# The start of an attention kernel: condition loaded first, its sigmoid from an exponential and a reciprocal, its factor on ScalarE

## The reference, cut to what matters

```
tf    = sigmoid(sum(cond, -1))
decay = exp(-exp(w)) * (0.5 + 0.5 * tf)
ek    = exp(min(f, 30));  ekv = ek * f
a forward and a backward scan  a = a * decay + ekv,  b = b * decay + ek
num   = nf + nb - ekv + euk * f;   den = df + db - ek + euk     with euk = exp(min(u + f, 30))
out   = sigmoid(x) * (num / max(den, 1e-8)) * (0.8 + 0.2 * tf)
```

## Time and profile before

| | us |
|---|---|
| median of 3 runs | 692.53 (692.39 to 693.21) |
| the profiled execution | 689.73 |
| its span, first to last instruction | 687.9 |
| TensorE busy in the span | 541.2 |
| VectorE busy | 407.4 |
| ScalarE busy | 373.0 |
| GpSimd busy | 147.5 |
| from the span's start to the first product of the attention | 33.88 |
| from the span's start to the first maxima | 48.04 |

### The profile page before, as it was taken

The page is one execution under the profiler, slowest core; times in us unless marked ns, Lnnn a source line. Parts: engine busy times, 40 slices in busy tenths (PEclk is TensorE's granted clock), DMA queues, the critical chain, the costliest instruction groups (busy, mean ns, idle before and its releaser), DMA issues.

```text
span 687.9 us, 13927 instructions
## 1 busy us (share of the span) xinstructions
PE 541.2 (79%) x5668; PEld 392.5 (57%) x5668; DVE 407.4 (59%) x612; ACT 373.0 (54%) x794; POOL 147.5 (21%) x115
## 2 busy tenths in 40 slices
PE   0097769778687766578999999999649999999980
PEld 0054445556455642353664656667648999996560
DVE  5889999999997477966655544454831111111223
ACT  6987788978876407555657555666322222222112
POOL 1000000000000127732019555520021222223110
PEclk9995699878868999899999999999759999999995
DMA  9500000000001000000000000000269999888825
GB/s 350 189 1 1 1 1 1 2 1 1 1 1 32 1 0 1 0 1 1 2 2 2 3 2 2 3 2 3 69 256 423 420 420 361 333 330 304 338 95 191
DMA packets 18480, 71.38 MB, mean 104 GB/s; under 512 B 4849, under 2 KB 9969, under 8 KB 14705
## 3 DMA queue, kind: packets, MB, share of 16 engines
q1 hardware_dynamic: 15408, 64.20, 24.5%
q0 software_dynamic: 1920, 5.25, 2.0%
q10 hardware_dynamic: 1088, 1.05, 0.5%
HBM read 65.77 MB, written 4.72 MB: 102 GB/s over the span
## 4 chain that ended last, share of the span: by engine, by line
PE 52%; DVE 31%; ACT 8%; issue 4%; DMA 3%; POOL 1%; SPq 0%; ACTq 0%; DVEq 0%; POOLq 0%
PE PS L1442 39%; DVE arena L942 4%; DVE nmx L1029 4%; DVE arena L939 4%; PE PS L1948 2%; PE PS L2017 2%; PE PS L1724 1%; PE PS L1589 1%; DVE R L956 1%; DVE arena L953 1%; DVE arena L954 1%; DMA arena<-in_moe 1%; DVE arena L948 1%; DVE arena L949 1%; ACT arena L773 1%
## 5 line engine op out<-in xcount | busy, mean ns | idle before, releaser
L1442 PE MATMUL PS<-arena 128*128 128x128 f32 (+6 forms) x1376 | 156.9, 291 | 17.6 <-DVE arena L1126 11.4
L1442 PEld LDWEIGHTS PS<-arena 128*128 128x128 f32 (+4 forms) x1376 | 125.8, 164 | 41.9 <-issue 25.0
L611 ACT ACTIVATE arena<-PS,nmx 128x128 f32<-128x128 f32 (+1 forms) x128 | 52.0, 422 | 32.6 <-DVE nmx L1029 32.6
L1390 DVE TENSOR_TENSOR R<-arena,PS 128x128 f32<-128x128 f32 x16 | 4.6, 288 | 88.1 <-ACT arena L870 88.1
L389 POOL TENSOR_SCALAR arena<-ident,gcol 128x128 f32<-128x128 f32 x4 | 2.4, 602 | 220.2 <-DMA gcol<-in_gcol 220.2
L449 POOL TENSOR_TENSOR arena<-arena 128x1024 f32<-128x1024 f32 x16 | 37.8, 2367 | 40.6 <-DVE arena L1208 32.5
L1506 PE MATMUL PS<-arena 32*128 32x128 f32 (+1 forms) x128 | 22.9, 438 | 29.9 <-ACT arena L611 29.6
L481 POOL DMA_INDIRECT ypair<-arena,oid x20 | 19.8, 988 | 121.8 <-ACT arena L876 121.8
L1442 PE MATMUL PS<-arena,R 128*128 128x256 f32 x192 | 44.2, 380 | 0.6 <-ACT arena L876 0.6
L1442 PEld LDWEIGHTS PS<-arena,R 128*128 128x128 f32 x192 | 35.2, 190 | 5.1 <-issue 1.0
L942 DVE TENSOR_TENSOR_SCAN arena<-dmat,arena 128x1023 f32<-128x1023 f32 x16 | 37.6, 2348 | 0.6
(11 more groups left out here) (306 smaller groups left out, 1198.3 us busy)
## 6 DMA issues: line engine op xcount, KB each, us to landing
arena<-in_moe SPq DMA_DIRECT2D x23, 1408.0 KB, 8.2
arena<-in_moe SPq DMA_DIRECT2D x23, 768.0 KB, 9.7
inproj<-in_inproj SPq DMA_DIRECT2D x1, 1344.0 KB, 10.5
arena<-in_fT SPq DMA_DIRECT2D x1, 1024.0 KB, 5.0
xT<-in_xT SPq DMA_DIRECT2D x1, 1024.0 KB, 5.4
R<-in_w1T SPq DMA_DIRECT2D x1, 1024.0 KB, 7.4
R<-in_w2T SPq DMA_DIRECT2D x1, 1024.0 KB, 9.4
R<-in_w3T SPq DMA_DIRECT2D x1, 1024.0 KB, 11.5
```

Source lines behind the costliest of these rows:

```text
L611: sc.activation(pr[u % 2][:, j, 0:n], PS[:, 2 * (u % 2) + j // 2, (j % 2) * 256:(j % 2) * 256 + n], ACT.Exp, bias=nmx[:, u % 2, j:j + 1], ...
L1442: last = mm(dst, l, r, start=(n == 0), stop=(n == len(pairs) - 1))
```

## The change

- **Loads.** `condT` is loaded first, with a semaphore of its own; `fT` comes in two loads, one for each half, with a semaphore each; `xT` goes behind the three feed-forward weights. `wu` is issued from ScalarE's queue, as the first thing in its program. `ones` and `notfirst` are not loaded any more: VectorE writes them with memsets, and also `tiny`, ahead of all its other work.
- **Sigmoid of the condition.** ScalarE takes `exp(-sum)`, in the table set of exponential and logarithm, which is now the first one loaded; VectorE adds one and takes the reciprocal.
- **First inputs.** The minimum with 30 is taken by half, behind `dq`. `fc = f * cb` is made by ScalarE (`by_condition`), two copies scaled by `cb` for each half. The scaled inputs of the first denominator scan (`ekq` of i = 0) are made by VectorE (`first_input`) instead of ScalarE's four copies.
- **ScalarE's order.** Decay of gate 0, exponential and factor of half 0, scaled values, bonus(0), exponential and factor of half 1, absolute sum 0, guess(0), absolute sum 1, the sigmoid's table, sigmoid of half 0, absolute sum 2, sigmoid of half 1, decay(1), scaled inputs (1,0), the three tanh, the queries, and only behind these the table of exponential and logarithm, the logarithm of `wtmp`, bonus(1) and the scaled inputs (1,1). The absolute sums write their unused output to `spent_abs`, words of the arena that the queries take later.
- **Names.** `pe_cond` and `pe_wsum` become `pe_sum` (1 and 2), `dve_ln` becomes the second count of `dve_winv`, `pool_pad` and `pool_diag` become `pool_made`.

```diff
-            load(fT, a["fT"], "f")
-            load(wu[:], a["wu"], "small")
-            load(condT[:], a["condT"], "small")
-            load(ones[:], a["ones"], "small")
-            load(notfirst[:], a["notfirst"], "small")
-            load(xT[:], a["xT"], "x")
+            load(condT[:], a["condT"], "cond")
+            load(fT[:, 0, :], a["fT"][:, 0, :], "f")
+            load(fT[:, 1, :], a["fT"][:, 1, :], "f1")
 
             for w, n in enumerate(("w1T", "w2T", "w3T")):
                 load(R[:, 1 + w].rearrange("p c n -> p (c n)"), a[n], "ffn")
+            load(xT[:], a["xT"], "x")
...
-            sc.preload_act_table(ACT.Sigmoid)
-            act.wait_ge(S["pe_cond"], 1)
-            sc.activation(tf[:], bank(7, B), ACT.Sigmoid).then_inc(S["act_cond"], 1)
+            act.dma_start(wu[:], a["wu"]).then_inc(ld["small"], 16)
             sc.preload_act_table_set(LN_EXP)
-            act.wait_ge(ld["small"], 64)
+            act.wait_ge(S["pe_sum"], 1)
+            sc.activation(tf[:], bank(7, B), ACT.Exp, scale=-1.0).then_inc(S["act_cond"], 1)
+            act.wait_ge(ld["small"], 16)
...
-            for ct in range(CT):
-                act.wait_ge(S["dve_fmin"], ct + 1)
-                sc.activation(ek[:, ct, :], ek[:, ct, :], ACT.Exp).then_inc(S["act_ek"], 1)
-                if ct == 0:
-                    scaled_inputs(0, 0)
-                decay(ct)
-                if ct == 0:
-                    scaled_inputs(0, 1)
+            def exp_inputs(c):
+                act.wait_ge(S["dve_fmin"], c + 1)
+                sc.activation(ek[:, c, :], ek[:, c, :], ACT.Exp).then_inc(S["act_ek"], 1)
+
+            def by_condition(c):
+                f4, s4 = (w[:, c, :].rearrange("p (a b t) -> p a b t", a=CT, b=B // NCH) for w in (fc, fT))
+                for b in range(B // NCH):
+                    last = sc.activation(f4[:, :, b, :], s4[:, :, b, :], ACT.Copy, scale=cb[:, 2 * c + b:2 * c + b + 1])
+                last.then_inc(S["act_ek"], 1)
...
-            bonus(0)
-            scaled_inputs(1, 0)
-            reciprocal_guess(0)
-
-            act.wait_ge(ld["ffn"], 48)
-            for w in range(3):
-                done(sc.activation(A[:].rearrange("p a n -> p (a n)"), R[:, 1 + w].rearrange("p c n -> p (c n)"), ACT.Abs,
-                                   accum_out=wabs[:, w:w + 1]), "act_wabs")
+            def absolute_sum(w):
+                done(sc.activation(spent_abs, R[:, 1 + w].rearrange("p c n -> p (c n)"), ACT.Abs, accum_out=wabs[:, w:w + 1]), "act_wabs")
...
-
+            decay(0)
+            exp_inputs(0)
+            by_condition(0)
+            act.wait_ge(S["dve_dec"], 2)
+            scaled_inputs(0, 1)
+            bonus(0)
+            exp_inputs(1)
+            by_condition(1)
+            act.wait_ge(ld["ffn"], 48)
+            absolute_sum(0)
+            reciprocal_guess(0)
+            absolute_sum(1)
+            sc.preload_act_table(ACT.Sigmoid)
             sigmoid_x(0, 0)
+            absolute_sum(2)
             sigmoid_x(0, 1)
-
+            decay(1)
+            scaled_inputs(1, 0)
             act.wait_ge(S["dve_winv"], 1)
             for w in range(3):
                 wv = R[:, 1 + w].rearrange("p c n -> p (c n)")
                 sc.activation(wv, wv, ACT.Tanh, scale=winv[:, w:w + 1]).then_inc(S["act_tanh"], 1)
-            sc.preload_act_table_set(LN_EXP)
-
-            act.wait_ge(S["dve_ln"], 1)
-            sc.activation(wat[:], wtmp[:], ACT.Ln).then_inc(S["act_atanh"], 1)
-            bonus(1)
-            scaled_inputs(1, 1)
             act.wait_ge(ld["attn"], 48)
...
             for mt in range(CT):
                 queries(0, mt, mt)
+            sc.preload_act_table_set(LN_EXP)
+            act.wait_ge(S["dve_winv"], 2)
+            sc.activation(wat[:], wtmp[:], ACT.Ln).then_inc(S["act_atanh"], 1)
+            bonus(1)
+            scaled_inputs(1, 1)
...
+            done(v.memset(ones[:], 1.0))
+            done(v.memset(notfirst[:], 1.0))
+            done(v.memset(notfirst[:, 0:1], 0.0), "dve_ones")
...
             dve.wait_ge(S["act_cond"], 1)
+            done(v.tensor_scalar(tf[:], tf[:], 1.0, None, ALU.add))
+            done(v.reciprocal(tf[:], tf[:]))
             done(v.tensor_scalar(hf[:], tf[:], 0.5, 0.5, ALU.mult, ALU.add))
             done(v.tensor_scalar(cb[:], tf[:], 0.2, 0.8, ALU.mult, ALU.add))
+            dve.wait_ge(S["act_exw"], 1)
...
+            smallest(0)
             done(v.reciprocal(rdq[:], dq[:]))
...
+            smallest(1)
+
+            def values_in(c):
+                dve.wait_ge(S["act_ek"], 2 * c + 2)
                 done(v.tensor_tensor(ekv[:, c, :], ek[:, c, :], fc[:, c, :], ALU.mult), "dve_fc")
+
+            def first_input():
+
+                dve.wait_ge(S["act_ek"], 1)
+                by_batch = [P, CT, B // NCH, T]
+                done(v.tensor_tensor(ekq.rearrange("p (a b t) -> p a b t", a=CT, b=B // NCH),
+                                     ek[:, 0, :].rearrange("p (a b t) -> p a b t", a=CT, b=B // NCH),
+                                     dq[:, 0, :, 0:B // NCH].unsqueeze(3).broadcast_to(by_batch), ALU.mult))
...
-            inputs(0)
+            first_input()
+            values_in(0)
...
-            inputs(1)
+            values_in(1)
```

More of the change, by code:

```diff
@@ L277, in bank @@
             return PS[:, i, 0:n]
-        ld = {k: sem("ld_" + k) for k in ("x", "f", "const", "small", "ffn", "attn", "ssd", "gb", "route")}
+        ld = {k: sem("ld_" + k) for k in ("x", "f", "f1", "cond", "const", "small", "ffn", "attn", "ssd", "gb", "route")}
         ld_ring = [sem(f"ld_ring{i}") for i in range(RING)]
@@ L389, in _ @@
                     last = pool.tensor_scalar(diagg[:, ct, l, :], ident[:], gcol[:, ct, l:l + 1], None, ALU.mult)
-            last.then_inc(S["pool_diag"], 1)
+            last.then_inc(S["pool_made"], 1)
             def roots(c):
@@ L899, in _, with smallest @@
             v = nc.vector
-            dve.wait_ge(ld["f"], 16)
-            for ct in range(CT):
-                done(v.tensor_scalar(ek[:, ct, :], fT[:, ct, :], 30.0, None, ALU.min), "dve_fmin")
-            dve.wait_ge(S["act_exw"], 1)
+            done(v.memset(ones[:], 1.0))
+            done(v.memset(notfirst[:], 1.0))
+            done(v.memset(notfirst[:, 0:1], 0.0), "dve_ones")
+            done(v.memset(tiny[:, 0:1], -1e-8))
+            done(v.memset(tiny[:, 1:2], 1e-8))
+            def smallest(c):
+                dve.wait_ge(ld[("f", "f1")[c]], 16)
+                done(v.tensor_scalar(ek[:, c, :], fT[:, c, :], 30.0, None, ALU.min), "dve_fmin")
             dve.wait_ge(S["act_cond"], 1)
+            done(v.tensor_scalar(tf[:], tf[:], 1.0, None, ALU.add))
+            done(v.reciprocal(tf[:], tf[:]))
             done(v.tensor_scalar(hf[:], tf[:], 0.5, 0.5, ALU.mult, ALU.add))
             done(v.tensor_scalar(cb[:], tf[:], 0.2, 0.8, ALU.mult, ALU.add))
+            dve.wait_ge(S["act_exw"], 1)
             done(v.tensor_tensor(dec[:], ew[:].unsqueeze(3).broadcast_to([P, 4, CT, B]),
@@ L913, in _ @@
             done(v.tensor_scalar(dq[:], dq[:], 1e-12, None, ALU.max), "dve_dec")
+            smallest(0)
             done(v.reciprocal(rdq[:], dq[:]))
-            done(v.memset(tiny[:, 0:1], -1e-8))
-            done(v.memset(tiny[:, 1:2], 1e-8))
-            dve.wait_ge(ld["small"], 64)
-            def tiles(w):
-                return w.rearrange("p (a b t) -> p a b t", a=CT, b=B // NCH)
-            def inputs(c):
-                bs = slice(c * B // NCH, (c + 1) * B // NCH)
-                done(v.tensor_tensor(tiles(fc[:, c, :]), tiles(fT[:, c, :]),
-                                     cb[:, bs].unsqueeze(1).unsqueeze(3).broadcast_to([P, CT, B // NCH, T]), ALU.mult))
-                dve.wait_ge(S["act_ek"], c + 1)
-                done(v.tensor_tensor(ekv[:, c, :], ek[:, c, :], fc[:, c, :], ALU.mult), "dve_fc")
+            smallest(1)
+            def values_in(c):
+                dve.wait_ge(S["act_ek"], 2 * c + 2)
+                done(v.tensor_tensor(ekv[:, c, :], ek[:, c, :], fc[:, c, :], ALU.mult), "dve_fc")
+            def first_input():
[4 more added lines that the diff above has]
+                                     dq[:, 0, :, 0:B // NCH].unsqueeze(3).broadcast_to(by_batch), ALU.mult))
             def gate_step(i, k):
@@ L970, in ternary_scales @@
                 done(v.tensor_scalar(wsc[:], wsc[:], 1.0, None, ALU.add))
-                done(v.tensor_tensor(wtmp[:], wtmp[:], wsc[:], ALU.mult), "dve_ln")
+                done(v.tensor_tensor(wtmp[:], wtmp[:], wsc[:], ALU.mult), "dve_winv")
             def keys(c, mt, b):
@@ L1445, in acc @@
                 return last
-            pe.wait_ge(ld["small"], 64)
-            acc(bank(7, B), [(ones[0:64, :], condT[:, :])], "pe_cond")
+            pe.wait_ge(ld["cond"], 16)
+            pe.wait_ge(S["dve_ones"], 1)
+            acc(bank(7, B), [(ones[0:64, :], condT[:, :])], "pe_sum")
             pe.wait_ge(S["act_wabs"], 3)
```

(4 more changed lines are left out.)

28 lines of the change are left out of this document (16 added, 12 removed).

## The result

The changed kernel has a median of 685.64 us over 7 runs (683.52 to 686.96); the kernel before, run beside it, 692.39 over 7 (688.95 to 693.21). The ratio is 0.991, with a 95% interval of 0.9884 to 0.9935: faster by 4.5 to 8.0 us. I had forecast 688.0 with a range from 686.4, so the time fell out of the range, on the fast side. The profiled executions took 684.17 after (span 682.3) and 689.73 before.

A forecast was written before the change was run, and what follows sets the result against it. VectorE's order of work was taken to set the attention, with everything changed in series ahead of it. First scan 3.2 us earlier plus stalls of 0.55 and 0.80 made 4.5 us: median 692.53 - 4.5 = 688.0, range 686.4 to 690.2.

The forecast's parts named there:

- What limits the kernel, and that a gain reaches the end: VectorE's order sets the attention; a microsecond saved before the first maxima at 48.04 is one off the end.
- Part 1: Condition at the kernel's start: `condT` issued first lands at 3.3, `dec` is done at 5.25 against 9.8 before.
- I take 3.3: Landing time of `condT` at the start, taken nearest to where data first flows at the full rate.
- The rule that I set beside it: Fixed DMA cost of about 2.0 us puts `condT` at 2.7: sum 0.6 better, median 687.4.
- the rival of a late condition: At the start, `condT` lands at 5.0 or `wu` at 5.2: 688.7 to 689.7, chance 0.11.
- parts 1 to 3: From the condition to gate (0,0): first scan 3.2 us earlier, stalls of 0.55 and 0.80 gone, 4.5 us in all.
- Parts 2 to 4: First inputs to first maxima: scan at 10.6, both stalls gone, products to maxima unchanged, maxima at 43.5; sum 4.5 us.
- the rival with a switch of twice that: ScalarE's table switch ahead of bonus(1) and `weigh(0)` costs twice 1.30, `weigh(0)` 1.2 late: 689.2, chance 0.03.
- The carrying to the median: At the end: the 4.5 us summed in the profiled execution is subtracted from the median 692.53, giving 688.0.
- the load, the pace and the table: Range terms: `condT` at 2.3 (1.0) or late, two more slow TensorE products (0.9), ScalarE's table switch (689.2).

The follow-up runs named there:

- e3: The changed kernel with `condT` loaded third, behind both halves of `fT`: median 688.39 us, ratio 0.9969 to the kernel before.
- e5: The changed kernel with ScalarE's old order of work; loads, condition and first inputs stay changed: median 688.37 us, ratio 0.9965 to the kernel before.
- e1: The kernel before, run again without edits: median 690.57 us, ratio 1.0003.
- e14: The kernel before with 12 unused products on TensorE behind the condition's sum: median 687.55 us, ratio 0.9957.
- e11: The changed kernel with 12 unused products on TensorE right behind the condition's sum, early: median 680.35 us, ratio 0.9834 to the kernel before.
- e6: The changed kernel with 12 unused products on TensorE shortly ahead of the gate, between 22.4 and 28.6 us: median 680.80 us, ratio 0.9857 to the kernel before.
- e9: The kernel of e6 once more, unchanged: median 678.18 us, ratio 0.9832 to the kernel before.
- e10: The kernel of e6 with ScalarE's scaled inputs (1,1) moved behind the first weights, `weigh(0)`: median 680.30 us, ratio 0.9847 to the kernel before.
- e13: The kernel of e11 with 64 unused products in place of 12, so 256 extra instructions: median 684.88 us, ratio 0.9922 to the kernel before.
- e8: The changed kernel with `ekv` of half 0 made by GpSimd, ScalarE's bonus(0) and second exponential ahead of its scaled values: median 685.62 us, ratio 0.9927 to before.

## Why the prediction was wrong

**What limits the kernel, and that a gain reaches the end.** Right: the 5.14 at the maxima came out in full, as 5.8 to 6.75 between medians side by side; e3's 3.3 at the condition were 3.7 in the median, e5's 2.95 at the maxima about 3.

**Part 1, a gain too small.** The failed step inside the sum is "I take 3.3" for the landing of `condT`. Its product started at 2.70, 0.6 earlier. The DMA rows of after show it:

```profile
R<-in_w3T SPq DMA_DIRECT2D x1, 1024.0 KB, 10.9
...
condT<-in_condT SPq DMA_DIRECT2D x1, 1.0 KB, 1.9
wu<-in_wu ACTq DMA_DIRECT2D x1, 8.0 KB, 1.6
```

1.9 us from the issue, against 4.3 behind 1 MB. I took the time at which data flowed at the full rate for a load of 1 KB, which needs no full rate; the first data moved at 2.25, and that was the nearer row. The rule that I set beside it, about 2.0 us fixed ("DMA: Bandwidth & Descriptors" of the Trainium skill, the two cost components), gave 2.7 and agrees with this trace. `wu` took 1.6 on ScalarE's queue, so the rival of a late condition had neither of its loads. All that follows in parts 1 to 3 keeps this 0.6 and adds almost nothing: `dec` done at 4.62 (5.25 forecast), first scan 9.93 (10.6), gate 27.30 (27.95).

**Parts 2 to 4.** Right in each step. The first half of `fT` was there when VectorE reached its minimum at 5.31; the second half released its minimum at 6.55, 0.15 late, hidden in the wait for ScalarE. Both stalls, 0.55 and 0.80, are gone, and the sigmoid was 2.6 ahead of its gate (2.4 forecast). The table load ahead of it took 1.28 with the next instruction 0.01 behind its end (22.37, 23.66), so the rival with a switch of twice that had no case. From products to maxima it took 14.23, against 14.16 before and 14.2 forecast, with 9.70 for the 16 products against 9.37. `weigh(0)` followed the maximum at 43.63.

**The carrying to the median.** This is the larger failure. "Median 692.53 - 4.5" put a difference from one profile on a median of three runs. The same kernel stood lower in most other runs: 689.73 profiled, 690.57 in e1, 690.1 to 691.6 beside the other experiments; the seven runs beside the result (median 692.39) lie over 4.3 us. The range held terms for the load, the pace and the table, and nothing for this spread, which alone is wider than its lower side of 1.6. From a start of 690.5, 690.5 - 4.5 is 686.0, and with the load at its measured place 685.4, against 685.64. That the start stood 2 too high is argued from the other runs and not shown for this one: beside the result the kernel before was at 692.39, and from there the 5.14 of the maxima leave 1.6 of the 6.75 unexplained. The ratio's interval of 4.5 to 8.0 us has the forecast 4.5 at its edge.

**What stays open.** What sets the spread of a kernel's executions isn't settled; the attention's length varies with waits for TensorE (180.7 to 182.8 in runs of before and after). Whether the change gives more than the 5.1 at the maxima isn't either: with the waits on issue gone in both kernels, the maxima of e14 and e11 lie 5.4 apart and the medians 7.2, though these two ran beside different runs of the kernel before. The waits on issue account for 2.7 to 3.8 of what e6, e9 and e11 gained on the kernel after. e3's profile has only 454.6 behind its attention with 2.7 of such waits in it, so something else also varies there by some 3 us.

The fastest kernels run are those with 12 idle products on the changed kernel (e6, e9, e10 and e11, 678.2 to 680.8). Their gain depends on the length of TensorE's program, and an edit to it can take it away, as e13's did.

## What to carry to other kernels

Load the few bytes that everything waits for first: alone they took 1.9 us, behind two loads of half a megabyte their product started 3.3 later, and all of it reached the first maxima and, as far as medians tell, the end. Before one forecasts a difference below one per cent, the time to subtract from must be a middle of many executions, and the range must hold the spread of single ones; a difference past the edited stage is compared with a second run of the unchanged kernel before it gets a reason. A difference far from the edit may also come from the number of instructions in an engine's program: adding idle ones, once a few and once a full 256, tells that apart, and so do the loads on the instruction queue, set beside the waits.

## What was not expected of the hardware

- TensorE waited 2.7 to 3.8 us in two waits on issue in the middle of dense small matmuls; 48 more instructions removed the waits, 256 put them back (3.2). Each wait ended 1.2 to 1.6 us behind the end of a 16,384-byte load of instructions.
- The same 16 products of 512 columns took 7.1 when TensorE had worked until 0.34 us or less before them (e6, e9), 8.80 behind a wait of 0.86 (e10), and 9.16 to 10.13 behind one of 1.09 or longer (all others). In these others TensorE had also stood idle for 6.9 us (e13) to 24.4 us (e8) ahead of the two small products of the weights' sums, so the last wait alone is not shown to be the cause. The granted clock doesn't tell it in every profile: over the first 3.5 us of these products it is 1.00 in the kernel after and 0.50, the 1.2 GHz level, in e11, with four products in each.

The stretches, of the kernel after and of e11 (length; TensorE, its weight loads, VectorE, ScalarE, GpSimd busy; granted clock; DMA share; GB/s):

```profile
28.70:32.20 3.50, 3.50 (x4) 1.46 (x5) 3.23 (x9) 3.50 (x7) 0.00 (x0) 1.00 0.00 0
```
```profile
28.70:32.20 3.50, 3.49 (x4) 1.49 (x5) 3.23 (x9) 3.50 (x7) 0.00 (x0) 0.50 0.00 0
```

- VectorE's product of four columns took 2.12 beside a GpSimd product, 0.17 without, and GpSimd's 4.41 instead of 2.37 (e8).
